# A graph convolution kernel whose ring of gathered rows gets seven places instead of five for a part of its run

## What is computed

```python
def _rgcn_conv(x, src, dst, etype, W, root, b):
    x_src = x[src]
    seg = dst * num_rel + etype
    sums = jax.ops.segment_sum(x_src, seg, num_segments=num_nodes * num_rel)
    cnt = jax.ops.segment_sum(jnp.ones((src.shape[0],)), seg, num_segments=num_nodes * num_rel)
    mean = (sums / jnp.maximum(cnt, 1.0)[:, None]).reshape(num_nodes, num_rel, -1)
    out = jnp.einsum('nri,rio->no', mean, W)
    return out + x @ root + b

h = relu(_rgcn_conv(x, src, dst, edge_type, W1, root1, b1))
out = _rgcn_conv(h, src, dst, edge_type, W2, root2, b2)
return _layernorm(x + out, axis=-1)
```

## Time and profile before

| | |
|---|---|
| median of 3 runs | 1489.88 us (1488.75 to 1493.27) |
| the profiled execution's own time | 1488.91 us |
| its span | 1487.2 us |
| TensorE busy | 1459.8 us (98%), 9044 matmuls |
| its weight loads | 1445.0 us (97%) |
| VectorE busy | 992.1 us (67%) |
| ScalarE busy | 577.5 us (39%) |
| GpSimd busy | 573.7 us (39%) |
| the products of line 810, three groups of 2100 matmuls | 707.7, 702.5 and 702.4 us (they overlap) |
| the gathers of line 547, 380 of them | 493.8 us busy, 1299 ns each, landing 4.8 us after issue |
| the chain that ended last | TensorE 75%, VectorE 9%, DMA 6%, GpSimd 5% |

### The profile page before, as it was taken

How to read it: one execution, slowest core, us unless ns; L and a number is a source line. 1 busy time by engine, 2 the same in 40 slices (tenths; PEclk the granted TensorE clock), 3 DMA queues, 4 the chain that set the end, 5 groups by cost and what they waited for, 6 DMA issues and landing times.

```text
span 1487.2 us, 24213 instructions
## 1 busy us (share of the span) xinstructions
PE 1459.8 (98%) x9044; PEld 1445.0 (97%) x9044; DVE 992.1 (67%) x1594; ACT 577.5 (39%) x828; POOL 573.7 (39%) x457
## 2 busy tenths in 40 slices
PE   8999999999999999999999999999999999999998
PEld 8999999999999999989999999999999999999997
DVE  8899899957777676888651054544445454448887
ACT  4222211134444444466352243334333343317654
POOL 0000000055678686766306142424242424315553
PEclk9999999999999999999999999999999999999999
DMA  6453221268777777466318474646465655625454
GB/s 204 137 176 117 90 75 42 75 199 256 245 206 229 230 240 215 140 184 196 104 48 258 134 226 142 215 146 214 157 200 173 187 187 170 226 75 154 143 165 135
DMA packets 109596, 249.72 MB, mean 168 GB/s; under 512 B 20183, under 2 KB 83334, under 8 KB 109442
## 3 DMA queue, kind: packets, MB, share of 16 engines
q0 software_dynamic: 32480, 135.65, 31.3%
q1 hardware_dynamic: 77026, 112.88, 23.3%
HBM read 204.47 MB, written 65.49 MB: 182 GB/s over the span
## 4 chain that ended last, share of the span: by engine, by line
PE 75%; DVE 9%; DMA 6%; POOL 5%; issue 3%; ACT 2%; SPq 0%; ACTq 0%; POOLq 0%; DVEq 0%
PE prod L810 59%; PE agg L856 11%; DMA raw<-y,bucket_index 4%; POOL raw L547 3%; PE agg L810 2%; DVE slot_hot L1361 2%; POOL scale L555 2%; DVE g_low L1100 1%; PE prod L801 1%; DVE keyed L1369 1%; DVE dst_hot L1362 1%; PE agg L976 1%; ACT g_high L665 1%; PE prod L856 1%; DVE g_low L1096 1%
## 5 line engine op out<-in xcount | busy, mean ns | idle before, releaser
L810 PE MATMUL prod<-w_high,h_high 128*128 128x384 f32 x2100 | 707.7, 337 | 0.7 <-DVE acc L1074 0.7
L810 PE MATMUL prod<-w_high,h_low 128*128 128x384 f32 x2100 | 702.5, 335 | 0.0
L810 PE MATMUL prod<-w_low,h_high 128*128 128x384 f32 x2100 | 702.4, 334 | 0.0
L547 POOL DMA_INDIRECT raw<-y,bucket_index x380 | 493.8, 1299 | 537.8 <-DVE g_low L1100 273.8
L1100 DVE TENSOR_TENSOR g_low<-raw,g_high 128x768 fp32r<-128x768 f32 x280 | 258.2, 955 | 333.8 <-ACT g_high L665 333.1
L698 ACT ACTIVATE y_stage<-prod 128x384 f32<-128x384 f32 x280 | 137.8, 492 | 677.5 <-PE prod L810 668.8
L810 PEld LDWEIGHTS prod<-w_high,h_high 128*128 128x128 f32 x2100 | 394.6, 188 | 0.9 <-issue 0.9
L810 PEld LDWEIGHTS prod<-w_low,h_high 128*128 128x128 f32 x2100 | 394.7, 188 | 0.0
L810 PEld LDWEIGHTS prod<-w_high,h_low 128*128 128x128 f32 x2100 | 394.3, 188 | 0.0
L665 ACT ACTIVATE g_high<-raw 128x768 fp32r<-128x768 f32 x300 | 240.3, 839 | 110.4 <-DMA raw<-y,bucket_index 61.3
L856 PE MATMUL agg<-g_high,one_hot 128*128 128x384 f32 x720 | 189.9, 345 | 12.8 <-DVE g_low L1100 10.4
(11 more groups left out here) (157 smaller groups left out, 874.6 us busy)
## 6 DMA issues: line engine op xcount, KB each, us to landing
y<-y_stage SPq DMA_DIRECT2D x280, 168.0 KB
w_raw<-in_w_all SPq DMA_DIRECT2D x35, 1152.0 KB
raw<-y,bucket_index POOLq DMA_INDIRECT x380, 4.8
y<-y_stage SPq DMA_DIRECT2D x280, 19.5 KB
y<-in_x SPq DMA_DIRECT2D x1, 3750.0 KB, 14.2
acc<-in_x POOLq DMA_DIRECT2D x10, 375.0 KB, 4.3
x_rows<-in_x SPq DMA_DIRECT2D x10, 336.0 KB
y<-acc SPq DMA_DIRECT2D x10, 336.0 KB
```

Of the source, the lines that this page charges most:

```text
L547: pool.indirect_dma_start(raw[:, i % NRAW, :], None, y[0:written * N, :], bass.IndirectOffsetOnAxis(ap=bucket_index[:, at_column:at_column ...
L810: mm = pe.matmul(to, left[:, k, t * P:(t + 1) * P], right[:, h, k, :], start=(k == 0 and left is h_high and right is w_high), stop=(n == 0 ...
```

## The change

The ring gets seven places for tiles 0 to 119. The two new places are the two tiles of `x_rows`. From tile 120 on, the ring has its five places again. The waits are worked out from which tile had a place last (`freed_by`) and how often the place was filled before (`loads_before`). `x_rows` is zeroed by GpSimd behind `raw`, and `spill_i` moves to the memory of `acc`. No instruction is added but that memset.

```diff
+    NWIDE = NRAW + 2
...
-        spill_i = at("spill_i", [EP, 4, EJ], i32, X0)
+        spill_i = at("spill_i", [EP, 4, EJ], i32, A0)
...
-        raw_loaded = [sem(f"raw_loaded{s}") for s in range(NRAW)]
+        raw_loaded = [sem(f"raw_loaded{s}") for s in range(NWIDE)]
...
+        PAIRED = BEHIND[R - 2]
+
+        def raw_slot(g, i):
+
+            n = behind(g) + i if isinstance(g, int) else LAYER + i
+            return n % NWIDE if n < PAIRED else (n - PAIRED) % NRAW
...
+        def freed_by(g, i):
+
+            if not isinstance(g, int):
+                return behind(g) + i - NRAW + 1
+            n = behind(g) + i
+            return 1 + max([m for m in range(n) if (m % NWIDE if m < PAIRED else (m - PAIRED) % NRAW) == raw_slot(g, i)],
+                           default=-1)
+
+        def raw_rows(slot):
+            return raw[:, slot, :] if slot < NRAW else x_rows[:, slot - NRAW, :]
...
-                pool.wait_ge(low_ready, behind(g) + i + 1)
-                pool.indirect_dma_start(raw[:, i % NRAW, :], None, y[0:written * N, :],
+                slot = raw_slot(g, i)
+                pool.wait_ge(low_ready, NRAW + freed_by(g, i))
+                pool.indirect_dma_start(raw_rows(slot), None, y[0:written * N, :],
...
             link(pool.memset(raw[:], 0.0))
+            link(pool.memset(x_rows[:], 0.0))
             pool.wait_ge(indexed, 1)
...
             def high_of_tile(g, i, column):
-                slot = i % NRAW
-                act.wait_ge(raw_loaded[slot], 16 * (behind(g) // NRAW + i // NRAW + 1) if isinstance(g, int)
-                            else (g - R) * (16 * PLAIN // NRAW) + 16 * (LAYER // NRAW + i // NRAW + 1))
+                slot = raw_slot(g, i)
+                act.wait_ge(raw_loaded[slot], 16 * (loads_before(g, i) + 1))
...
-                    rows, high = raw[p:P, i % NRAW, :], g_high[p:P, split_slot(g, i), :].bitcast(f32)
+                    rows, high = raw_rows(raw_slot(g, i))[p:P], g_high[p:P, split_slot(g, i), :].bitcast(f32)
```

More of the change, by code:

```diff
@@ L283, in tile_range, with loads_of, loads_before @@
             return range(start, start + tiles(g))
+        PAIRED = BEHIND[R - 2]
+        def raw_slot(g, i):
+            n = behind(g) + i if isinstance(g, int) else LAYER + i
+            return n % NWIDE if n < PAIRED else (n - PAIRED) % NRAW
+        def loads_of(slot, n):
+            return sum(m % NWIDE == slot for m in range(min(n, PAIRED))) + \
+                sum((m - PAIRED) % NRAW == slot for m in range(PAIRED, n))
+        def loads_before(g, i):
+            if isinstance(g, int):
+                return loads_of(raw_slot(g, i), behind(g) + i)
+            return (g - R) * (PLAIN // NRAW) + loads_of(raw_slot(g, i), LAYER + i)
+        def freed_by(g, i):
[6 more added lines that the diff above has]
+            return raw[:, slot, :] if slot < NRAW else x_rows[:, slot - NRAW, :]
         def one_before(g, t):
@@ L550, in gather_tile @@
                                         bounds_check=row_limit, oob_is_err=False)\
-                    .then_inc(raw_loaded[i % NRAW], 16)
+                    .then_inc(raw_loaded[slot], 16)
             def load_scale(i):
@@ L661, in high_of_tile @@
                     act.wait_ge(scale_loaded, 16 * T * BLOCKS)
-                    act.activation(g_high[:, split_slot(g, i), :], raw[:, slot, :], ACT.Copy, scale=scale[:, column:column + 1])\
+                    act.activation(g_high[:, split_slot(g, i), :], raw_rows(slot), ACT.Copy, scale=scale[:, column:column + 1])\
                         .then_inc(high_ready, 1)
                 else:
-                    act.activation(g_high[:, split_slot(g, i), :], raw[:, slot, :], ACT.Copy).then_inc(high_ready, 1)
+                    act.activation(g_high[:, split_slot(g, i), :], raw_rows(slot), ACT.Copy).then_inc(high_ready, 1)
             def bucket(g, t):
```

## The result

| | before | after |
|---|---|---|
| median | 1493.27 us (1488.75 to 1496.0, 7 runs) | 1486.16 us (1484.93 to 1489.71, 7 runs) |
| ratio | | 0.9958, 95% interval 0.9945 to 0.9971 |
| profiled execution, own time / span | 1488.91 / 1487.2 us | 1484.97 / 1483.2 us |

The kernel got faster: by 4.0 us from span to span, by 7.1 us from median to median, and by 0.42% in the ratio, which is 6.3 us, where 10.0 us were forecast. The time of 1486.16 us lies 6.3 us above the forecast, outside the forecast's own range of 1477.5 to 1482.5 us and inside the range for 8 in 10. The forecast started from a median of 1489.88 us over 3 runs; beside the changed kernel, over 7 runs, that median was 1493.27 us.

A forecast was written before the change was run, and what follows sets the result against it. TensorE, busy 98% of the span, bounds the kernel. Gain 10.8 - 0.5 - 0.3 = 10.0 us from 1488.9 gives 1478.9, and the median 1.0 above: 1479.9 us; own range 1477.5 to 1482.5, 8 in 10 1476 to 1487.

The forecast's parts named there:

- what bounds: Three products with pairs of sums: TensorE waits 8.7 us for gathers landing late beside weight loads; 10.6 us of lead needed.
- Not bytes: Rival: gathers issued earlier still queue behind the same weight loads; gain 0 to 3 us, here 1488.5 us; chance 0.10.
- what sets the lead: The ring holds back the first product's late gather; later, GpSimd needs 4.66 us a step against TensorE's 4.54.
- the leads after: Late tiles' leads with seven places: 13.0 us in the first product, 13.5 and 12.7 at the end, 11.0 if issues slow.
- The 0.5 us that I kept for the last tile's wait: End of the third product: 0.5 us of wait counted as staying, as GpSimd's slower issues cut the lead to 11.0 us.
- the rate rival: GpSimd's issue rate is the bound, so the waits at 552.03 and 596.25 us stay: 1483.4 us; chance 0.12.
- the parts at nothing: Extra memset (1.3 us, up to 0.3 more) hidden by GpSimd's idle time, moved spill_i, return to five places: each 0.
- the gross gain: Three products: five landing waits 8.4 us, overlap 1.0 us, bucket at half clock 1.4 us; together 10.8 us.
- what is late next: ScalarE's copy into y_stage in step 19, waiting for a store behind the weight load: 0.3 us in all.
- the store of step 15 in the second product: Its landing behind the weight load delays ScalarE's copy of step 19: 0 to 1.3 us, 0.3 taken.
- The slower rival: Stores land later, ScalarE holds TensorE up: decides from a 13.6 us landing, 1494.5 us from 15.1 on; chance 0.05.
- The signs: Profile after, 335 to 590 us: TensorE's waits fall from 8.7 to about 1 us, no half clock, store waits in all products.

The follow-up runs named there:

- run 5: Kernel before (five places) without the six weight loads of the three products with pairs of sums, old weights used: 1485.25 us, ratio 0.9947.
- run 1: Kernel after (seven places) measured once more, no edit: 1478.01 us, ratio 0.9922.
- run 3: Kernel after with six ring places instead of seven: 1478.75 us, ratio 0.9922.
- run 10: Kernel after, seven places, with the weight load of step 14 issued behind the stores of steps 15 and 16: 1481.28 us, ratio 0.9939.
- run 6: Kernel before (five places) without GpSimd's 40 lookups of scales, which are set to 1: 1479.7 us, ratio 0.9921.
- run 2: Kernel after with five ring places again, memset, moved spill_i and new waits kept: 1490.25 us, ratio 0.9996.
- run 9: Kernel after measured again, unchanged, on another chip than its first repeat: 1483.41 us, ratio 0.9964.
- run 7: Kernel before (five places) with the weight load of step 14 issued behind the stores of steps 15 and 16: 1491.21 us, ratio 0.9987.
- Run 8: Kernel after with an extra 1152 KB HBM-to-HBM copy just ahead of each load of step 14 in the three products: 1504.23 us, ratio 1.0072.
- run 4: Kernel after, seven places, with the weight load of step 14 issued behind the stores of steps 15 and 16: 1477.41 us, ratio 0.9912.
- run 11: Kernel after with six places and the weight load of step 14 behind the stores of steps 15 and 16: 1482.06 us, ratio 0.9950.

## Why the prediction was right and wrong

**Right: what bounds.** Run 5 (no loads, no such waits) and run 1 (same gathers, longer leads, landings of up to 8.8 us, no wait) bear out that a gather beside a weight load can need 8.6 us and comes too late with a lead of 7.5 to 8.5 us. Not bytes but the time of the issue decided. The 8.6 us were the slowest of one execution, though: run 3 has a landing of 9.4 us and run 10 one of 10.8 us.

**Right: what sets the lead.** Without the lookups (run 6) the four later waits went and the first product's stayed: there the ring held the gather back, and behind it GpSimd's three issues a step.

**Right, at the safe end: the leads after.** I counted 13.5 and 12.7 us at the last tiles before any slowing of GpSimd, and 11.0 for the last behind it. Measured were 14.0 us for the last (571.81 to 585.78). The slowing did not come. GpSimd by line from 408 to 598 us in run 1:

```profile
L578 POOL DMA_INDIRECT raw<-y,bucket_index x58 | 69.1, 1191 | 33.2 <-DMA y<-y_stage 14.1 <-issue 13.4 <-DVE g_low L1131 5.4
L586 POOL DMA_INDIRECT scale<-inv_table,scale_index x37 | 46.0, 1244 | 11.3 <-issue 10.7 <-DVE g_low L1131 0.6
L578 POOL DMA_INDIRECT x_rows<-y,bucket_index x22 | 25.9, 1179 | 7.9 <-issue 4.9 <-DVE g_low L1131 3.0
```

A gather took (69.1 + 25.9) / 80 = 1.19 us and a lookup 1.24, so a step needs 2 x 1.49 + 1.54 = 4.52 us, no longer more than TensorE's 4.54. I had let it rise with VectorE's share, which did rise, from 0.71 to 133.95 / 178 = 0.75 (408 to 586 us). The 0.5 us that I kept for the last tile's wait was not there. In the kernel after, a gather took 1.29 us instead (69.3 and 27.4 us for 75), and its lead still sufficed. So the rate rival did not decide here. Its 1483.4 us lies nearer to the result than the forecast, by chance: the waits that it priced did not come.

**Right: the parts at nothing.** Memset (1.38 us here), `spill_i`, and the return to five places, by run 2. For the memset 1.3 to 1.6 us was counted, and GpSimd's idle time ahead of the next ring entry shrank from 12.58 to 9.39 us.

**Too small: the gross gain.** 10.8 us were counted, with 0.29 and 0.16 us of the first product's store left standing. Run 1 gained 12.2 us in the three products, 0.9 more than all of these. A half-clock stretch of 3.4 us costs 1.7 us and not the 1.4 that I read from its first bucket. The remaining 0.6 us is not assigned. Over the 10.8 us that were counted, the gain is 1.4 us more.

**Wrong: what is late next.** This is the step that failed: the term for what is late next was 0.3 us, and the kernel after paid 6.9 us. I took 0.3 us for the store of step 15 in the second product, by the nearest row, with 1.3 us as the upper end. The kernel after paid 1.69 us there and, behind it, 1.7 us at 1.2 GHz, and 1.82 + 1.7 us for a copy that the sum did not hold. Three things were wrong in it:

- The landing: 10.3 us was read from one execution and carried over. The runs show 9.7 us in run 1 (486.14 to 495.8) and 11.6 us in the kernel after, and the threshold of 4.7 us of waiting lies between them. The load stood at the same distance from the product's end each time, 8.2 us (394.63 to 402.86 in the kernel before, 485.70 to 493.94 in run 1, 486.03 to 494.26 in the kernel after), so the landing alone made the difference. Over five profiles ScalarE waited 4.44 (run 6), 4.50 (run 1), 4.67 (run 3), 5.68 (run 9) and 6.42 us (the kernel after) for this store in the second product. A term that hangs on a threshold wanted the spread of its cause, not its last value.
- The stretch at half clock. I had seen one behind the wait of 2.17 us, booked it as a gain, and did not book it for a wait that might take the place of the old ones.
- The copy behind a late signal of TensorE. A copy that ran 2 to 5 us late for that reason was not in the trace of before, so the sum had no term for it. In the kernel after it cost 1.82 + 1.7 = 3.5 us. That the ring brings it out is not shown: with five places it cost as much, 1.93 and 1.66 us of waiting in run 7 and 1.89 and 1.95 us in run 5, each with a stretch of 3.4 us behind it. So this half of the miss may be no effect of the change at all.

Together these are 6.9 us, less the 0.3 counted. The forecast of 1478.9 us for the profile, plus these 6.6, less the 0.5 not needed, less the 1.4 us more of gross gain, is 1483.6 us. The first product of the kernel after also began 2.0 us later than before (310.9 against 308.9), of which 1.7 us is one more stretch at 1.2 GHz near 259 us, ahead of all that the change touches, and the work behind the products was 0.9 us shorter. That gives 1484.7 us; the profile has 1485.0. From profile to profile the miss is therefore explained to 0.3 us. The median of the runs lies 1.2 us above the profile, where 1.0 us was counted.

**The slower rival had the right place and the wrong price.** It asked for a landing of 13.6 us before the gain was eaten. Run 8 shows the mechanism, 1 us for 1 us beyond the threshold, plus the clock, which stood at 0.50 for 6.8 and 10.2 us there. Below that point it does not lose the gain but takes a part of it, and for this middle case, some 3 to 7 us dearer than the forecast, I had no chance written down.

**The signs.** As written, the landing waits are gone and ScalarE's waits for them too. "No stretch at clock 0.50" and "about 1 us of waits" failed in the kernel after and held in run 1. Of the waits for the store of step 15 "in all three products" run 1 shows one and run 3 all three. The signs of being wrong, issues above 1.30 us and stores later than 12 us, were not reached in the kernel after (1.29 and 11.6 us), and yet the forecast missed. The third sign, a wait of over 1 us for a landing beside a load, came once with seven places, in run 10.

**Open.** The copy behind a late signal of TensorE stands in no profile of the kernel before and of runs 1 to 4. It stands in six of the other eight: in that of the kernel after and in those of runs 5, 7, 8, 9 and 10, not in 6 and 11. Of 13 such copies 12 lie in steps 11 to 14 of the second or third product, with five places and with seven, with and without weight loads. Each of the 13 starts 0.02 us behind the update of the semaphore that its product's last matmul raises, and that update comes 1.7 to 5.2 us behind the matmul's end. Why the signal is late stays open; the ends of matmuls are modelled, and these eight profiles all lack some of the semaphore updates (13.2 to 13.9 thousand of DMAs, where the other five have 16.8 thousand). The profile of the kernel before is of the complete kind and that of the kernel after is not, so the two need not differ by the ring alone. I can't say either whether the smaller gain (0.9958 and 0.9964 against 0.9922) belongs to the chip or to chance; each of these intervals is from one chip.

## What to carry to other kernels

To price a deeper ring, take the lead (issue to use) of every late entry and compare it with the slowest landing, of several executions if there are any (8.6 us in one, 10.8 us in another here), and find out for each whether the ring or the issuing engine's rate holds it back; that part held to within 1.5 us. Then price what comes next by its threshold: read how long the next waiting instruction may wait before the bound engine feels it (here 4.7 us), and put the spread of its cause against that, since a value just below it says nothing of the next execution. Where the bound engine's clock falls behind waits, book the lost time behind the new waits as well as behind the old.

## What the runs showed of the hardware that I had not expected

- Waits of TensorE of 1.5 to 2.5 us in these products were followed by 3.4 us at 1.2 GHz in 9 of 22 cases over all the profiles. Length does not tell them apart: one of 1.66 us was followed by it, one of 2.27 us (run 6) was not, and in run 2 such a stretch began at 555.18 us, behind waits of only 0.87 and 0.66 us. In run 9 the clock stayed at 1.00 behind the wait of 1.75 us, as this window shows:

```profile
471.60:475.00 3.40, 3.37 (x19) 3.24 (x20) 3.40 (x6) 1.47 (x3) 2.94 (x2) 1.00 0.76 231
```

  Each such stretch is worth 1.7 us, as much as the wait ahead of it.
- A gather's issue by GpSimd got longer with fewer issues around it: 1.24 us before, 1.385 us in run 6, where the lookups were gone, and 1.19 us in run 1. It does not follow GpSimd's own load but VectorE's splits (`g_low` and `w_low`, which read two tiles). In these three profiles and that of the kernel after, from 408 to 598 us, 126 gathers were issued beside none of them and took 0.99 to 1.02 us each. All 144 issues of over 1.1 us ran beside a split. In run 6, where a split releases most gathers, 48 of 81 ran beside one, and those took 1.65 us on average.
- One kernel's medians on two chips were 1478.01 and 1483.41 us, while the kernel before had 1490.89 and 1490.3 us on them. A gain of 12.9 us on one was 6.9 us on the other.
